# A two-layer graph transformer on one core: twelve sorted blocks in layer 1, with fewer VectorE operations per unit and per node tile

## What is computed

```python
src = concatenate([src, loops]); dst = concatenate([dst, loops])      # every node has an edge to itself
for l in range(2):
    xn = layernorm(x, ln1_g[l], ln1_b[l])
    deg = segment_sum(ones, src); deg = (deg - deg.mean()) / (std(deg, ddof=1) + 1e-6)
    xp = xn + xn @ Wpos[l] + bpos[l] + deg[:, None] * Wdeg[l][0] + bdeg[l]
    q, k, v = xp @ Wq[l] + bq[l], xp @ Wk[l] + bk[l], xp @ Wv[l] + bv[l]      # 8 heads of 16
    att = clip(einsum('ehd,ehd->eh', q[dst], k[src]) / 4, -50, 50)
    ex = exp(att - segment_max(att, dst)[dst])
    aggr = segment_sum(v[src] * ex / segment_sum(ex, dst)[dst], dst)
    x = x + aggr @ Wo[l] + bo[l]
    x = x + gelu(layernorm(x, ln2_g[l], ln2_b[l]) @ W1[l] + b1[l]) @ W2[l] + b2[l]
return layernorm(x0 + x)
```

## Time and profile before

| | |
|---|---|
| median of 3 runs | 3647.36 us (3645.29 to 3647.68) |
| span of the profiled execution | 5559.9 us |
| instructions in it | 72300 |
| busy in it: PE, PEld | 3461.6 us, 2666.6 us |
| busy in it: DVE, ACT, POOL | 2916.7, 1771.1, 2472.4 us |
| TensorE clock granted, mean share of full speed | 0.744 |
| DMA | 548.28 MB, 20.9% of 16 engines' span by the gathers' queue, 11.9% by SP's |

### The profile page before, as it was taken

One profiled execution on the slowest core, in us unless ns is written; L12 is line 12 of the kernel. 1 busy time (PEld: TensorE's weight loads), 2 busy tenths in 40 slices (PEclk: granted clock), 3 DMA queues, 4 the chain that ended last, 5 costly groups with the idle time before them and its releaser, 6 DMA issues.

```text
span 5559.9 us, 72300 instructions
## 1 busy us (share of the span) xinstructions
PE 3461.6 (62%) x24196; PEld 2666.6 (48%) x24475; DVE 2916.7 (52%) x6780; ACT 1771.1 (32%) x4391; POOL 2472.4 (44%) x2597
## 2 busy tenths in 40 slices
PE   5834656655665656666566376666666566666666
PEld 4623445444454445444444254455555455545545
DVE  9944545554454545555455354554554454545455
ACT  2301232323333332323234133333333333333334
POOL 1065444444444444444542544445444454444443
PEclk7756777777777777777777677777777777777777
DMA  2133333333333333333332333333333333333332
GB/s 73 49 111 87 88 106 93 102 88 95 102 94 99 94 102 89 104 95 96 107 105 65 106 103 109 108 107 113 96 108 106 108 110 113 111 102 115 109 104 73
DMA packets 404556, 548.28 MB, mean 99 GB/s; under 512 B 78348, under 2 KB 318656, under 8 KB 403988
## 3 DMA queue, kind: packets, MB, share of 16 engines
q0 software_dynamic: 123648, 337.81, 20.9%
q1 hardware_dynamic: 273030, 198.56, 11.9%
q10 hardware_dynamic: 7506, 7.20, 0.4%
HBM read 518.00 MB, written 25.29 MB: 98 GB/s over the span
## 4 chain that ended last, share of the span: by engine, by line
PE 32%; another core or an unknown queue 30%; DVE 14%; issue 12%; ACT 10%; DVEq 0%; SPq 0%; DMA 0%; ACTq 0%
PE psum L952 7%; PE psum L993 4%; PE psum L1009 3%; ACT scratch L1227 3%; PE psum L1042 3%; PE psum L1026 3%; DVE att L1685 2%; PE psum L970 2%; ACT arena L1238 2%; DVE scratch L1676 2%; DVE kv_ring L1394 1%; PE psum L1123 1%; DVE work L1377 1%; DVE scratch L1700 1%
## 5 line engine op out<-in xcount | busy, mean ns | idle before, releaser
L1971 POOL DMA_INDIRECT kv_ring<-kv_table,src_idx x1936 | 1846.4, 954 | 2132.8 <-DVE scratch L1700 1501.1
L1227 ACT ACTIVATE scratch<-psum 128x512 f32<-128x512 f32 x1148 | 649.5, 570 | 2061.3 <-remote 1442.0
L952 PE MATMUL psum<-arena 128*128 128x256 f32 x1764 | 631.5, 486 | 464.2 <-issue 194.2
L1971 POOL DMA_INDIRECT arena<-kv_table,src_idx x640 | 607.8, 950 | 664.6 <-DVE scratch L1700 489.7
L1726 DVE SCALAR_TENSOR_TENSOR arena<-psum,in_block,arena 128x136 f32 x644 | 200.9, 353 | 1286.4 <-remote 1187.3
L993 PE MATMUL psum<-q_win,scratch 64*128 64x128 f32 x5152 | 534.3, 349 | 285.7 <-issue 149.9
L952 PEld LDWEIGHTS psum<-arena 128*128 128x128 f32 x1764 | 372.6, 236 | 621.0 <-issue 319.2
L1009 PE MATMUL psum<-scratch 128*64 128x136 f32 x5152 | 519.1, 330 | 185.4 <-issue 154.2
L993 PEld LDWEIGHTS psum<-q_win,scratch 64*128 64x128 f32 x5152 | 443.2, 243 | 343.1 <-issue 332.5
L1238 ACT COPY arena<-psum 128x512 f32<-128x512 f32 x504 | 265.1, 532 | 986.9 <-remote 524.7
L1685 DVE TENSOR_REDUCE att<-scratch 128x64 f32<-128x1024 f32 (+1 forms) x448 | 525.1, 1172 | 0.1
(11 more groups left out here) (251 smaller groups left out, 4873.9 us busy)
## 6 DMA issues: line engine op xcount, KB each, us to landing
arena<-kv_table SPq DMA_DIRECT2D x126, 896.0 KB
kv_ring<-kv_table,src_idx POOLq DMA_INDIRECT x1936
q_win<-q_table SPq DMA_DIRECT2D x644, 32.0 KB
work<-kv_table SPq DMA_DIRECT2D x98, 128.0 KB
arena<-kv_table,src_idx POOLq DMA_INDIRECT x640
q_win<-q_table SPq DMA_DIRECT2D x126, 64.0 KB
work<-q_table SPq DMA_DIRECT2D x98, 64.0 KB
kv_table<-work SPq DMA_DIRECT2D x49, 128.0 KB
```

The costliest lines, as they stand in the source:

```text
L952: mm = e.matmul(to[:, t % 2 * 2 * D:(t % 2 + 1) * 2 * D], hot_source[:, t * P:(t + 1) * P], source_rows[:, t, :], start=True, stop=True)
L1227: e.activation(to[:, at:at + width], apart[k % 2][:, 0:width], ACT.Relu, bias=1.0, scale=-1.0).then_inc(apart_read, 1)
L1971: e.indirect_dma_start(kv[m % RING_KV][:, t, :], None, kv_table[l], bass.IndirectOffsetOnAxis(ap=src_idx[:, c * T + t:c * T + t + 1], axis ...
```

## The change

Layer 1 does twelve tiles by blocks for ten, so it has 149 chunks for 157, 84 blocks for 70 and four sorts for two; between two blocks there may now be a single chunk. `kv_block` has two buffers. The ring of windows shrinks from 32 to 16 and `AHEAD` from 8 to 4, which makes the room for it. `make_products` is one operation for a unit, over both banks of spread queries. The Newton step has two operations on VectorE, with a third value, -0.5 (v + eps), from ScalarE. The sort's `tensor_reduce` writes bf16 itself, without the cast. The bias row goes into PSUM by a product of one row, and the degree row and TensorE's product are added in one operation. The count of the start covers two more tiles (13 steps). The diff, cut to its core:

```diff
-NBS = 8, 10
+NBS = 8, 12
-RING_W = 32
-AHEAD = 8
+RING_W = 16
+AHEAD = 4
-        assert all(b - a > 2 for a, b in zip(self.block_at, self.block_at[1:]))
+        assert all(b - a > 1 for a, b in zip(self.block_at, self.block_at[1:]))
-        kv_block = part_of(TB * 2 * D).rearrange("p (t d) -> p t d", t=TB)
+        kv_blocks = [part_of(TB * 2 * D).rearrange("p (t d) -> p t d", t=TB) for _ in range(2)]
...
+                e.matmul(ps[:, 0:QKV], ones[0:1, :], b_next[0:1, :], start=True, stop=False)
-                e.matmul(ps[:, 0:QKV], col, w_qkv[:, l + 1, :], start=True, stop=True).then_inc(done, 1)
+                e.matmul(ps[:, 0:QKV], col, w_qkv[:, l + 1, :], start=False, stop=True).then_inc(done, 1)
...
-            if m >= 1 and i == 0:
-                e.wait_ge(msg_ready, block_unit(m - 1) + 1)
+            if m >= 2 and i == 0:
+                e.wait_ge(msg_ready, block_unit(m - 2) + 1)
...
             e.activation(tiny[:, 8:9], tiny[:, 7:8], ACT.Ln, bias=small[:, 0:1]).then_inc(norm_log, 1)
+            e.activation(tiny[:, 10:11], tiny[:, 7:8], ACT.Identity, scale=-0.5, bias=small[:, 1:2])
...
-            for h in range(2):
-                f = 2 * n + h
-                ...
-                e.wait_ge(spread, f + 1)
-                ...
-                e.tensor_tensor(prod[:, ts[0] * P:(ts[-1] + 1) * P].rearrange("p (t d) -> p t d", d=D),
-                                q_edge[f % 2][:, 0:len(ts) * P].rearrange("p (t d) -> p t d", d=D), keys, ALU.mult
-                                ).then_inc(prod_ready, 1)
+            e.wait_ge(spread, 2 * n + 2)
+            e.tensor_tensor(prod[:, 0:ts * P].rearrange("p (t d) -> p t d", d=D),
+                            q_edges[:, 0:ts * P].rearrange("p (t d) -> p t d", d=D), keys, ALU.mult
+                            ).then_inc(prod_ready, 2)
...
-                    e.tensor_reduce(whole, s_sel.rearrange("p b g -> p g b"), AX_X, ALU.add).then_inc(sort_picked, 1)
-                    e.wait_ge(sort_picked, 3 * (SA * s + q) + 2)
-                    e.tensor_copy(by_run(s_rank)[:, q], whole).then_inc(sort_picked, 1)
+                        e.tensor_reduce(by_run(s_rank)[:, q], s_sel.rearrange("p b g -> p g b"), AX_X, ALU.add
+                                        ).then_inc(sort_picked, 1)
...
-            step(e.scalar_tensor_tensor, out=t, in0=v, scalar=EPS, in1=y, op0=ALU.add, op1=ALU.mult)
-            step(e.scalar_tensor_tensor, out=t, in0=t, scalar=-0.5, in1=y, op0=ALU.mult, op1=ALU.mult)
+            step(e.scalar_tensor_tensor, out=t, in0=y, scalar=minus_half, in1=y, op0=ALU.mult, op1=ALU.mult)
             step(e.scalar_tensor_tensor, out=y, in0=t, scalar=1.5, in1=y, op0=ALU.add, op1=ALU.mult)
...
-            elif k == 29:
-                e.scalar_tensor_tensor(out=qkv, in0=wz_next[:], scalar=deg_z[:, j:j + 1], in1=b_next[:], op0=ALU.mult,
-                                       op1=ALU.add).then_inc(deg_row, 1)
             elif k == 31:
-                e.wait_ge(deg_row, LAYERS[l].pos[j] + 1)
-                e.tensor_tensor(qkv, ps("qkv")[:, 0:QKV], qkv, ALU.add).then_inc(qkv_ready, 1)
+                e.scalar_tensor_tensor(out=qkv, in0=wz_next[:], scalar=deg_z[:, j:j + 1], in1=ps("qkv")[:, 0:QKV],
+                                       op0=ALU.mult, op1=ALU.add).then_inc(qkv_ready, 1)
```

More of the change, by code:

```diff
@@ L342, in graph_transformer @@
         part_64 = sb("part_64", [P, 1])
-        small = sb("small", [P, 1])
+        small = sb("small", [P, 2])
         window = sb("window", [1, NC], I32)
@@ L1697, in make_messages @@
             ts = LAYERS[l].tiles_of(u)
-            values = kv[chunk(l, i) % RING_KV][:, :, D:2 * D] if what == "chunk" else kv_block[:, :, D:2 * D]
+            values = (kv[chunk(l, i) % RING_KV] if what == "chunk" else kv_blocks[part_number(l, i) % 2])[:, :, D:2 * D]
             e.wait_ge(exp_ready, n + 1)
@@ L1769, in sort_vector @@
                 elif k == 8 + 3 * q and q < SA:
[L1770 to L1774 removed]
+                    e.wait_ge(sort_picked, 2 * (SA * s + q) + 1)
+                    with nc.allow_low_precision(reason="one of the terms is a whole number up to 128, the others are 0"):
+                        e.tensor_reduce(by_run(s_rank)[:, q], s_sel.rearrange("p b g -> p g b"), AX_X, ALU.add
+                                        ).then_inc(sort_picked, 1)
                 elif k == 9 + 3 * q and q < SA:
[L1776 removed]
+                    e.wait_ge(sort_picked, 2 * (SA * s + q) + 2)
                     if SA * s + q:
```

41 lines of the change are left out of this document (19 added, 22 removed).

## The result

The changed kernel takes 3843.9 us (median of 4 runs, 3830.9 to 3849.8) against 3646.3 (3644.0 to 3647.7): a ratio of 1.054, with a 95% interval of 1.0517 to 1.0564 (in brackets from here on): **198 us slower**. The forecast was 3610 us, with a range up to 3690.

A forecast was written before the change was run, and what follows sets the result against it. The prediction took GpSimd's gather issue to set the pace in both layers, with TensorE second. 3647 us, less 40 in layer 1, plus 3 at the start, gave 3610, range 3562 to 3690.

The forecast's parts named there:

- the pace of layer 1: Layer 1's edges: 1377 us of TensorE work at density 0.90 takes 1530 us, down from 1570, so -40.
- the signs named for the forecast: In layer 1, TensorE's waits shrink and GpSimd waits for messages there; no size given.
- Rival C: Layer 1: TensorE's in-order queue is the bound below density 0.877; at 0.85, 3700 us in all; chance 0.24.
- Rival B: Layer 1: TensorE keeps density 0.92 and GpSimd rules, full gain of 80 us, 3570 in all; chance 0.25.
- Rival D: Lost gathers and added blocks cancel, 3647 us within 7, or the program takes its far slower general path; chance 0.11.
- Merged product: Query product in one operation: saves 68 us of VectorE, nothing on the path; 77 us if other fills don't cover it.
- Bias row: Layer 0: one-row product adds 32 to 65 us of TensorE, hidden under GpSimd's 1650; VectorE saves 30.
- Newton's steps: 196 norms: dropping one 0.156 us operation and its wait saves 37 us of VectorE, which hides.
- ring of 16: Window ring, 4 ahead: some 17 chunks of slack, so costed at nothing.
- Start: Start before the edges: VectorE's count runs 13 steps for 11, +3 us, which shows.
- Source rows: Layer 1's 23 close pairs of blocks wait for the single source-row buffer: 0 to 46 us, inside the density.
- SBUF port: Gathers beside VectorE's sorting operations slow from 0.95 to 1.49 us: 0 to 6 us more for GpSimd.

The follow-up runs named there:

- run 77: Not a run: "run" is a verb here; twelve stretches of two chunks with a sort take 77 us more than their gathers.
- before again: The kernel before, unchanged, profiled again for a trace beside the changed kernel's; span 3651.2 us.
- half picks: Changed kernel with the value half of the blocks' row products on TensorE left out in both layers; 3779 us.
- half copies: Changed kernel with ScalarE copying only the keys of a block's rows from the third block on; 3799 us.

## Why the prediction was wrong

**The step that failed** is the pace of layer 1: "I take the middle, 0.90". The work was right: +128 us at full clock forecast, +129 of busy time measured (estimate and measure count the clock differently, so the closeness is in part luck). The gathers were right: 80 us less to issue. But 1377 us of work took 1742, a density of 0.79, and that is the density of before (1249 / 1576 = 0.79). I had read that 0.80 as what the gathers asked for, with room above it up to 1.00, because single stretches of 4 us were full. There was little room: with eight blocks there are no waits in layer 1, with eleven 76 us of them, at a density of 0.82 (1313 / 1605). That after comes to the very 0.79 of before is chance, for in before the gathers set it. Part of what is missing to 1.00 is the clock: of 1742 us, 343 were at half clock, and TensorE was busy 0.82 of the time. Of the signs named for the forecast, GpSimd's waits for messages came, but TensorE's waits grew (275 to 312 us idle) where they should have shrunk. The end that I had written down for 0.80, 1721 us and +151, is what came (+165); I left it out of the range, which stopped at 3690.

**Why a mean density misleads.** The sum set layer 1's whole work against its whole gathers. The gathers run ahead by what the ring holds, and the imbalance is local: a block with one chunk needs 14.1 us of TensorE and 10.0 of GpSimd, and no stretch of three chunks is left to make up for it. From figures of the prediction (8.4 + 2.76 + a share of the node tiles, 196 / 84 = 2.3) such a stretch comes to 13.5 us; it could have been seen. The same holds for the sorts: 64 us of TensorE's 1377 looked small, but they stand in 16 stretches, and the twelve of them with two chunks run 77 us over their gathers.

**Rival C** had the place and the sign right and the size wrong: it put 0.85 beside a threshold of 0.877, 3700 us, with a chance of 0.24. **Rival B** leaned on TensorE's weight loads. They are busy 1134 us of 1742 in layer 1 of after, 65%, while the matmuls are busy 1430 and GpSimd waits for the edge work. The Trainium skill (Trainium Kernel Development and Optimization, "Performance Expectations") calls weight-load time, beside the share of peak FLOPs reached, a good measure of how close a kernel is to its roofline, and matmul time a bad one. Read as room for more work, as rival B read it, the 65% would leave a third of the engine free; here it does not predict the bound. **Rival D** fell by the time; the plan took its fast path, with the 2,512 gathers foreseen.

**Merged product:** "so nothing on the path" failed; it costs 11 us beside ten blocks and 28 beside twelve, where the bound for an uncovered wait was 77. The wait it adds is the one named. The saving was oversized too: 68 us forecast, but the two halves overlapped, so VectorE's busy time in those lines falls from 560.7 to 535.4 us over the two layers, with 6 more units to do.

**Bias row:** 46.8 us of TensorE measured, inside "32 to 65"; "so 65 more hides" failed, for it costs 15.5 us. GpSimd did wait 26 us in layer 0 of before: layer 0 is not wholly gather-paced either, and its 1695 us are 1320 x 1.255 = 1657 and some 38 of waits and long gathers.

**Newton's steps:** 92 to 74 us of busy time and 6 less idle, 24 us for the forecast 37. **Newton, ring of 16, second buffer, sort** together cost nothing, as said (3645.2 us at ten blocks, 6 under before); no run has one of them alone. **Start:** +3 forecast; 285.4 in after and 287.6 in before again, with 280.7 to 301.4 over the traces of changed kernels, so it can't be told. **Source rows:** 0 to 46 us forecast, 25.9 us of waits seen, 5 us worth. **SBUF port:** the longest gather apart from the first ones is 1.54 us and the median is 946 ns for 947; with twice the sorts in layer 1 its gathers' mean is 951 for 950: no cost.

**Layer 0** changed by 13 us, over the 10 that I had named as a sign of error, though traces of the same layer 0 differ by up to 15. The product and the bias row, 11 and 15.5 us, are enough to explain it. **The tail** was taken as unchanged; it grew by 15.5 us, and is 44 us in the traces with ten blocks, 50 with eleven and 60 with twelve.

**What stays open:** why the stretches with two chunks are 22.2 us long beside twelve blocks and 21.0 beside eleven. They have 0.75 us more idle time and 2 us more at half clock; no run separated the two. Nor did a run separate the blocks of the two further tiles from their two sorts, or keep two chunks between all blocks. A third spare bank was not tried.

## What to carry to other kernels

When one engine's issue hides another's work, the hidden engine's share says nothing about its room: run the neighbouring sizes (here eight, ten, eleven, twelve) and see where the pacing engine begins to wait. Balance the two over the shortest stretch that the ring can't bridge, not over the layer, with what stands there besides (here the sorts). An operation merged or moved "because the engine has room" adds its wait to the round trip: here two such edits cost 11 to 28 and 15 us while saving 20 to 30 us on an engine that wasn't the bound.

## What the runs showed of the hardware

One chip ran everything about one and a half times as long: 5571.6 us for the kernel before, which takes 3651 elsewhere. Eleven blocks, half picks and half copies, 1.5 to 4.1% above before elsewhere, were 0.0 to 0.3% from it there, and eight blocks 1.5% for 2.5%; the granted clock was 0.75 (eleven blocks, over the whole span) for 0.89. The cause was not found, and a comparison there alone would have hidden the slowdown of these three.

A VectorE operation on 128x1 with constants as its scalars took 157 ns mean (588 of them before). Of the two steps left, taken in pairs from the trace of after, the first, whose scalar is read from memory, took 215 ns and the second, with a constant, 164 (196 of each): fewer steps saved less than their number. That the scalar from memory is why is likely and not shown, as no run changed it alone.

TensorE took 157 us of unneeded products in layer 1 with no change in the time of the kernel (3846.5 us for 3843.9). TensorE had been idle for 312 us there; beside the products the granted clock was 0.96 for 0.90, and the other products were busy some 105 us less (157 less the 52 by which busy time grew).
